# A graph kernel's attention messages: plain scatter into rows sorted by source block, summed by one-hot matmuls, in place of accumulating scatters

## The reference

```python
agg = segment_sum(xt[rel, src], dst)                 # both relational layers
...
scores = einsum(q[src], k[tgt]) / sqrt(16) + (curv @ Wc + bc)
probs  = segment softmax of scores over the edges of one tgt
messages = (probs[:, :, None] * v[tgt]).reshape(E, 128)
out = zeros_like(x).at[src].add(messages)            # sum by SOURCE node
out = out @ Wo + bo
x = x + out;  x = x + relu(LN(x) @ W1 + b1) @ W2 + b2
```

## Time and profile before

| | |
|---|---|
| device time, 3 runs | 12659.14 us median (12644.38 to 12664.75) |
| profiled execution, first to last instruction | span 10613.6 us |
| median less span | 2045.5 us |
| busy in the span | PE 57%, PEld 49%, DVE 53%, ACT 22%, POOL 70% |
| DMA | 851.83 MB, mean 80 GB/s |

### The profile page before, as it was taken

The page is one execution under the profiler, slowest core; times in us unless marked ns, Lnnn a source line. Parts: engine busy times, 40 slices in busy tenths (PEclk is TensorE's granted clock), DMA queues, the critical chain, the costliest instruction groups (busy, mean ns, idle before and its releaser), DMA issues. The chain is left out here.

```text
span 10613.6 us, 158173 instructions
## 1 busy us (share of the span) xinstructions
PE 6021.4 (57%) x25681; PEld 5185.3 (49%) x25682; DVE 5665.5 (53%) x14970; ACT 2361.1 (22%) x6137; POOL 7417.5 (70%) x6720
## 2 busy tenths in 40 slices
PE   0544444446444444434888898865666666666646
PEld 0333333333333333333888888854555555555544
DVE  5333333333333333335888888886555555555538
ACT  0100000001000000002555555532222222222222
POOL 1477777773777777761777777756888888888870
PEclk9655555556555555556555555556666666666667
DMA  1821111123111111112555555534555554444444
GB/s 38 292 71 52 52 52 52 52 52 132 52 52 52 52 52 52 52 52 80 136 136 136 135 137 135 136 92 62 58 58 59 59 59 58 59 59 59 58 58 120
DMA packets 1001820, 851.83 MB, mean 80 GB/s; under 512 B 187420, under 2 KB 892572, under 8 KB 1001707
## 3 DMA queue, kind: packets, MB, share of 16 engines
q0 software_dynamic: 400608, 439.19, 23.9%
q1 hardware_dynamic: 521299, 350.81, 11.7%
q10 hardware_dynamic: 79872, 61.39, 2.4%
HBM read 636.48 MB, written 234.17 MB: 82 GB/s over the span
## 5 line engine op out<-in xcount | busy, mean ns | idle before, releaser
L553 POOL DMA_INDIRECT stage_msg<-xt,stage_index x3328 | 3194.9, 960 | 1334.7 <-issue 924.8
L568 PE MATMUL stage_ps_agg<-stage_hot,stage_msg 128*128 128x128 f32 x6656 | 1714.7, 439 | 2522.8 <-DMA stage_msg<-xt,stage_index 2291.1
L1285 POOL DMA_INDIRECT sums<-big,stage_index x1664 | 2578.4, 1550 | 656.9 <-issue 397.0
L568 PEld LDWEIGHTS stage_ps_agg<-stage_hot,stage_msg 128*128 128x128 f32 x6656 | 1481.7, 328 | 2756.8 <-DMA stage_msg<-xt,stage_index 1402.2
L591 DVE TENSOR_TENSOR big<-big,stage_ps_agg 128x128 f32 x3328 | 957.8, 288 | 2388.6 <-PE stage_ps_agg L568 1985.0
L922 POOL DMA_INDIRECT big<-q,stage_index x1664 | 1600.0, 962 | 752.8 <-issue 443.0
L543 ACT ACTIVATE stage_index<-big 128x4 int32 x832 | 170.8, 205 | 4027.7 <-PE stage_ps_agg L568 4008.1
L1323 PE MATMUL stage_ps_val<-nodes_a,big 128*128 x3328 | 834.0, 430 | 332.7 <-ACT big L1267 216.9
L1357 DVE TENSOR_TENSOR big<-stage_ps_val,stage_prob 128x512 f32<-128x512 f32 x416 | 287.7, 692 | 1273.7 <-PE stage_ps_val L1323 1272.4
L1323 PEld LDWEIGHTS stage_ps_val<-nodes_a,big 128*128 128x128 f32 x3328 | 714.6, 317 | 381.8 <-issue 381.8
L1311 PE MATMUL stage_ps_src<-ident,stage_srcs 128*128 128x128 f32 x1664 | 367.8, 360 | 885.9 <-ACT stage_srcs L1256 750.5
(11 more groups left out here) (220 smaller groups left out, 7852.7 us busy)
## 6 DMA issues: line engine op xcount, KB each, us to landing
big<-in_edge_attr_dram SPq DMA_DIRECT2D x1664, 64.0 KB
xt<-big SPq DMA_DIRECT2D x26, 2048.0 KB, 6.6
stage_msg<-xt,stage_index POOLq DMA_INDIRECT x3328
stage_trow<-targets ACTq DMA_DIRECT2D x416, 128.0 KB
stage_trow<-targets SPq DMA_DIRECT2D x416, 128.0 KB, 3.3
sums<-stage_zero SPq DMA_DIRECT2D x104, 256.0 KB
big<-q,stage_index POOLq DMA_INDIRECT x1664
sums<-big,stage_index POOLq DMA_INDIRECT x1664
```

What stands on the lines that cost most here:

```text
L553: pool.indirect_dma_start(msg[q][:, j, :], None, xt, bass.IndirectOffsetOnAxis(ap=index[q][:, j:j + 1], axis=0))\
L568: last = nc.tensor.matmul(ps[q % 2][:, j, :], msg[q][:, j, :], hot[q % 2][:, j, :], start=True, stop=True)
L1285: pool.indirect_dma_start(d["sums"][h * G + j], bass.IndirectOffsetOnAxis(ap=index[q][:, j:j + 1], axis=0), total[q][:, j * D:(j + 1) * D] ...
```

## The change

1. **Slots.** Each valid or padding edge gets a row of its own in a DRAM table `slots` (212,992 rows of 528 B: 128 values, the source's number, three zeros). The edges are taken in 8 parts of 52 groups; within a part, rows are sorted by source block (`src >> 7`, 49 blocks). The first `aggregate` counts the edges of each block for each group, the second computes each edge's row; both load a broadcast list of blocks (`lanes`) once for each group.
2. **Plain scatter.** Messages go straight from DVE into `total`, whose rows POOL writes with four plain indirect transfers to a group. The search for repeats, the matmul within the tile and the copy are gone.
3. **Sums.** When a part has landed, SP loads its rows back, 5 tiles of 128 rows to a set, 52 sets to a part; a (tile, block) pair that straddles is loaded twice. PE multiplies each tile with a one-hot matrix of places in the block, DVE adds the five results to two accumulators in SBUF. This runs beside the groups of the next part, 56 groups behind (FIRST); the last part's 52 sets and four more turns follow the last group.
4. **Tables** that say which tile and block each load has are made on DVE and PE in groups 4 to 15 of `scatter`.
5. **Moves.** The loads of `targets`, `exp` and `marks` go from SP's queue to ACT's. `finish` takes the two accumulators from SBUF with two accumulating matmuls. The clearing of `sums` is gone.

```diff
+PARTS = 8
+GP = GROUPS // PARTS            # 52
+SET = 5
+LAG = SLOTS
+FIRST = GP + LAG                # 56
+SETS = PARTS * GP               # 416
+ROW = D + 4
 def aggregate(...):   # SP
-            for r in range(REP):
-                for a in range(BATCHES):
-                    sp.dma_start(d["sums"][r][...], zero[:, :]).then_inc(s_zd, 16)
+            if x.live(-SLOTS):
+                sp.wait_ge(s_counted if first else s_own, x.at(-SLOTS) + 1)
+            sp.dma_start(lanes[q][:, :], d["buckets"][...].partition_broadcast(W)).then_inc(s_lanes[q], 16)
+        if first:
+            for h in range(H):
+                sp.dma_start(d["marks"]...[:, h, :], d["tile_marks"]).then_inc(s_mk, 16)
+        walk(sp, group, 0, 0)
 # aggregate, DVE, in each group
+                if first:
+                    v.wait_ge(s_lanes[q], x.turn() * 16 + 16)
+                    nc.vector.tensor_scalar(met[h][:, :], lanes[q][:, :], t["lane"][0:W, :], 0.0, ALU.is_equal,
+                                            ALU.add, accum_out=t["counts"][:, bass.ds(x.at(), 1)])
+                else:
+                    nc.vector.tensor_tensor_scan(run[h][:, :], ones[:, :], own[h][:, :],
+                                                 begin[:, bass.ds(x.at(), 1)], ALU.mult, ALU.add)
...
+                    nc.vector.tensor_tensor(pick[h][:, :], run[h][:, :], own[h][:, :], ALU.mult)
 # scatter, SP
+        def load(y):
+            if y.live(-SLOTS):
+                sp.wait_ge(s_sum, y.at(-SLOTS) + 1)
+            r = windows(nc, mybir.EngineType.SP, pair_row, y.at() * SET, SET, K - 1)
+            for j in range(SET):
+                sp.dma_start(rows[q][:, j, :], d["slots"][bass.ds(r[j] * P, P), :]).then_inc(s_rows[q], 16)
+        for a in range(PARTS):
+            for q in range(SLOTS):
+                sp.wait_ge(s_sc[q], at[q] + (a + 1) * (GP // SLOTS) * (16 * G))
 # scatter, POOL
-                pool.indirect_dma_start(d["sums"][h * G + j], ..., total[q][:, j * D:(j + 1) * D], None,
-                                        compute_op=ALU.add).then_inc(s_sc[h], 16)
+                    pool.indirect_dma_start(d["slots"], ..., total[q][:, j, :], None).then_inc(s_sc[q], 16)
 # scatter, PE
-                for j in range(G):
-                    last = nc.tensor.transpose(ps_q[h][...], srcs[h][:, j:j + 1].to_broadcast([P, P]), ...)
-                for j in range(G):
-                    last = nc.tensor.matmul(ps_o[h][...], same[x.slot(-1)][:, j, :], msg[h][...])
+                for j in range(SET):
+                    last = nc.tensor.matmul(ps_s[h][:, j * P:(j + 1) * P], rows[q][:, j, 0:D], hot[h][:, j, :])
 # scatter, DVE
-                nc.vector.tensor_tensor(same[...], of_tiles(ps_q[h][:, :]), srcs[h]..., ALU.is_equal)
-                nc.vector.tensor_scalar(away[h]...)
-                nc.vector.tensor_tensor(dup, same[...], t["earlier"]..., ALU.mult)
-                nc.vector.tensor_reduce(dups[h]...)
-                nc.vector.scalar_tensor_tensor(moved[h]...)
-                nc.vector.tensor_tensor(dest[...]...)
+            if x.sums(1):
+                nc.vector.tensor_tensor(place[h][:, :], rows[q][:, :, D], pair_off[...], ALU.subtract)
+                v.wait_ge(s_place, x.at(1) + (1 - FIRST))
+                nc.vector.tensor_tensor(hot[h][:, :, :], t["iota"]..., place[h]..., ALU.is_equal)
+            if x.sums(-1):
+                w = windows(nc, mybir.EngineType.DVE, pair_window, (x.at(-1) - FIRST) * SET, SET)
+                v.wait_ge(s_sum, x.at(-1) + (1 - FIRST))
+                for j in range(SET):
+                    into = sums[j % 2][:, bass.ds(w[j] * P, P)]
+                    if j >= 2:
+                        v.wait_ge(s_acc, (x.at(-1) - FIRST) * SET + (j - 1))
+                    nc.vector.tensor_tensor(into, into, ps_s[h][:, j * P:(j + 1) * P], ALU.add)
 # finish, PE
-                    last = nc.tensor.matmul(ps_a[...], ot[:, j, :], wo_sb[:, :], start=True, stop=True)
+                    for c, sums in enumerate((t["nodes_b"], t["nodes_c"])):
+                        last = nc.tensor.matmul(ps_a[...], sums[:, ...], wo_sb[:, :], start=(c == 0), stop=(c == 1))
```

More of the change, by code:

```diff
@@ L501, in walk, with __init__, within, edge @@
         body(Group(g // slots, g % slots, slots, groups))
-def aggregate(nc, m, t, d, zero_sums):
+class Spot(Group):
+    def __init__(self, i, q, near):
+        super().__init__(i, q, SLOTS, None)
+        self.near = near
+    def within(self, k, lo, hi):
+        return lo <= self.near + k < hi
+    def edge(self, k=0):
+        return self.within(k, 0, GROUPS)
+    def live(self, k=0):
+        return self.edge(k)
+    def sums(self, k=0):
+        return self.within(k, FIRST, LAST)
+    def fixed(self):
+        return isinstance(self.i, int)
+def walk_edges(engine, body, marks, reach, lead):
+    g = marks[0] - reach
+    for a, b in zip(marks, marks[1:]):
+        first, end = -(-(a + (reach if a else lead)) // SLOTS), (b - reach) // SLOTS
+        if end - first < 2:
+            continue
+        for e in range(g, first * SLOTS):
+            body(Spot(e // SLOTS, e % SLOTS, e))
+        with engine.Fori(first, end) as i:
+            for q in range(SLOTS):
+                body(Spot(i, q, first * SLOTS + q))
+        g = end * SLOTS
+    for e in range(g, marks[-1] + reach):
+        body(Spot(e // SLOTS, e % SLOTS, e))
+def aggregate(nc, m, t, d, first):
     index = [m.sb(f"index{q}", [P, G], I32) for q in range(SLOTS)]
@@ L546, in _ @@
+        walk(act, group, 0, 0 if first else 6, peeled=1 if first else 2)
+        if not first:
+            act.wait_ge(s_kept, GROUPS)
     @block.gpsimd
@@ L560, in _, with group @@
         pe.sem_inc(s_freed, SLOTS)
-        with pe.Fori(0, TURNS) as i:
-            for q in range(SLOTS):
-                g = i * SLOTS + q
-                pe.wait_ge(s_hot, g + 1)
-                pe.wait_ge(s_read, g + 1)
-                pe.wait_ge(s_msg[q], i * (16 * G) + (16 * G + at[q]))
+        if not first:
+            pe.wait_ge(s_link, 1)
+            nc.tensor.matmul(ps_first[0:W, 0:PARTS], t["before"][0:W, 0:W], t["part_count"][:, :],
+                             start=True, stop=True).then_inc(s_first, 1)
+            pe.wait_ge(s_ones, 2)
+        def group(x):
+            if x.live():
+                q = x.slot()
+                pe.wait_ge(s_hot, x.at() + 1)
+                pe.wait_ge(s_read, x.at() + 1)
+                pe.wait_ge(s_msg[q], x.turn() * (16 * G) + (16 * G + at[q]))
                 for j in range(G):
@@ L570, in _ @@
                 last.then_inc(s_freed, 1)
+            if not first and x.live(-2):
+                h = x.slot(-2, 2)
+                pe.wait_ge(s_pick, x.at(-2) + 1)
+                if x.live(-4):
+                    pe.wait_ge(s_kept, x.at(-4) + 1)
+                for j in range(G):
+                    last = nc.tensor.matmul(ps_slot[h][:, j:j + 1], pick[h][:, j * P:(j + 1) * P], one[:, :],
+                                            start=True, stop=True)
+                last.then_inc(s_slot, 1)
+        walk(pe, group, 0, 0 if first else 2)
     @block.vector
@@ L1293, in _ @@
-        walk(pool, group, 0, 0)
-        for h in range(2):
-            pool.wait_ge(s_sc[h], TURNS * 2 * 16 * G + at[h])
+            if x.edge():
+                q = x.slot()
+                pool.wait_ge(s_index, x.at() * 2 + 2)
+                ring_index(pool, s_msg, x.at() + 1, passed)
+                for j in range(G):
+                    pool.indirect_dma_start(d["slots"], bass.IndirectOffsetOnAxis(ap=index[q][:, j:j + 1], axis=0),
+                                            total[q][:, j, :], None).then_inc(s_sc[q], 16)
@@ L1297, in _ @@
+        walk_edges(pool, group, (0, GROUPS), 0, SLOTS)
+        for q in range(SLOTS):
+            pool.wait_ge(s_sc[q], TURNS * 16 * G + at[q])
     @block.tensor
@@ L1336, in _ @@
-        walk(pe, group, 1, 1)
+            if x.sums():
+                h, q = x.slot(0, 2), x.slot()
+                pe.wait_ge(s_rows[q], x.turn() * (16 * SET) + (1 - FIRST // SLOTS) * (16 * SET))
+                pe.wait_ge(s_hot, x.at() + (1 - FIRST))
+                if x.sums(-2):
+                    pe.wait_ge(s_acc, (x.at() - (FIRST + 1)) * SET)
+                for j in range(SET):
+                    last = nc.tensor.matmul(ps_s[h][:, j * P:(j + 1) * P], rows[q][:, j, 0:D], hot[h][:, j, :],
+                                            start=True, stop=True)
+                last.then_inc(s_sum, 1)
@@ L1515, in batch @@
                 last.then_inc(s_y, 1)
-        walk(pe, batch, 1, 0, 2, BATCHES)
+        for g in range(-1, BATCHES):
+            batch(Group(g // 2, g % 2, 2, BATCHES))
     @block.gpsimd
@@ L1634, in build @@
             "xl": nc.dram_tensor("xl", (NP, D), FP32).ap(),
-            "sums": [nc.dram_tensor(f"sums{r}", (NP, D), FP32).ap() for r in range(REP)],
+            "slots": nc.dram_tensor("slots", (K * P, ROW), FP32).ap(),
         }
```

499 lines of the change are left out of this document (301 added, 198 removed).

## The result

The changed kernel takes 12940.5 us (median of 4), the kernel before 12651.8 beside it: ratio 1.0215, 95% interval 1.0176 to 1.0255, 2% slower. Forecast were 12175 us and a range of 11900 to 12620.

What follows compares the result with a forecast made beforehand. POOL was taken to bound `scatter` alone and `aggregate` by a thin margin. Terms -816 (scatter), +243 (tail), +45 and +105 (aggregates), -5 (prepare), -56 (finish) sum to -484: 12175 us, range 11900 to 12620.

Steps and rivals of the forecast that it cites:

- The ground: Whole kernel: profiled span 10613.6 us against a median of 12659.1; the 2045.5 us between them carried over unchanged.
- the sum: Whole kernel: -816 + 243 + 45 + 105 - 5 - 56 = -484 us, giving span 10130 and time 12175 us.
- Scatter, -816: `scatter` loop: plain writes at 1.0 us make DVE the bound, 5.5 us to a group; 2271 us in place of 3087.
- First aggregate, +45: First `aggregate`: `lanes` waits behind the copies of `marks`, so POOL stops after about six groups; +45 us, between 0 and 80.
- Second aggregate, +105: Second `aggregate`: DVE's added scan and product slow gathers that start inside them; +105 us, 20 or 310 at the ends.
- DVE's chain in my sum: Second `aggregate`: scan, `pick`, `hot` and four additions take DVE 4.85 us to a group, barely below POOL's 5.06.
- Tail, +243: After the last group of `scatter`: 52 sets served by SP at 4.5 us each, 234 plus 9; 190 or 260 otherwise.
- Finish, -56: `finish`: batches at 14.4 us in place of 18.24, and -7 for the first batch; -56 us, -30 to -110.
- A: Rival: POOL paces everything, `scatter` at 5.06 us to a group; total -735, 11925 us; chance 0.15.
- B: Rival: a plain write in `scatter` costs 1.27 us, 6.3 us to a group; -134, 12525 us; chance 0.14.
- C: Rival: indices on a write's DRAM side cost 1.55 us, not the addition; `scatter` stays at 7.42; +332, 12990 us; chance 0.12.

Runs made afterwards that it cites:

- the free run: The changed kernel, unchanged, a third time, where nothing stalls, beside the kernel before: 10300.3 us against 10609.0, ratio 0.9701.
- run 22060: Not a run's number: 22060 counts packets in the free run, the changed kernel, unchanged, against the kernel before: 10300.3 us, ratio 0.9701.

## Why the prediction was wrong

**The ground.** The step that failed is the first: "The 2045.5 us between them I carry over unchanged; no row shows what lies in them." They lay in the loops: 534 and 556 us in the two `aggregate` stages, 900 in `score`. So the earlier trace rows gave the pace of loops that the timed executions did not have, and a stage that was free of stalls before was taken to stay free. The new `scatter` did not stay so: 3160 us stalled, 2384 free. Without this error the sum would still have been too good, -298 us of span for -484, by the terms that follow.

**Scatter, -816.** Measured: +73 stalled, -701 free. The mechanism holds where nothing stalls: plain writes at 1.0 us, DVE the new bound, its register reads ahead of the additions. The size is 5.81 us for 5.5; the missed term is the read of five words, 1.20 us where I had taken the 0.34 of four. It is partly given back by the additions, which follow at 0.22 us, not 0.29, and by the steps before `hot`, 1.77 us and not 2.04. Of the first 56 groups, those from the 16th on went at 5.06 us, below the 5.2 of the sum, and the 12 in which the tables are made at 6.47. Stalled, the period is 7.76. Old `scatter` had 7.42 us of POOL's work to a group; the new one puts 42 instructions on DVE's queue and 28 on SP's (19.5 and 11 before), most of them register work, and both queues stall. Removing SP's reads, DVE's and both gives 0.1, 0.4 and 1.07 us of the 1.95 that the stalls cost; the rest is not traced to one queue.

**First aggregate, +45.** +57 stalled, +83 free; the stop came as told, but was 66 us stalled and 59 free for 50. At 83 us the term lies just beyond the 80 that I gave as its end.

**Second aggregate, +105.** +102 free, and by its mechanism: the gathers that meet DVE's longer operations go from a mean of 962 to 1023 ns (forecast 1.02 us). In free executions, before and after:

```profile
L553 POOL DMA_INDIRECT stage_msg<-xt,stage_index x1663 | 1599.1, 962 | 635.8 <-issue 465.7 <-ACT stage_index L543 170.1
L648 POOL DMA_INDIRECT stage_msg<-xt,stage_index x1663 | 1700.9, 1023 | 635.9 <-issue 437.9 <-ACT stage_index L618 198.0
```

The section on who interferes with whom of the page "SBUF — State Buffer" in the Trainium skill says that a VectorE instruction with two SBUF inputs contends with a GpSimd instruction that reads SBUF. The 962 and 1023 ns agree with it. The terms of DVE's chain in my sum add to 4.34 us, not to the 4.85 written there; both lie below POOL's 5.06, so nothing hung on it. Stalled the new operations cost nothing (-6 us): the group loses its 1.3 us with and without them, and POOL has time to spare.

**Tail, +243.** 298 us stalled, 288 free, each from the last group's writes on. The reason is that above: SP's read takes 1.07 us, a set 5.5 to 5.7 and not 4.5. Tail and `finish` together are +241 and +231 for the +187 of the sum.

**Finish, -56.** 292 us, from the last group's writes on, to 236 us after the tail: right in sum. A batch takes 16.1 us, not 14.4 (the 13 begin from 12710.4 to 12903.2), against the 18.24 of the earlier trace rows; the shorter start before the first batch gave the rest.

**Rivals.** A's condition (DVE under 5.06 us) and B's price (1.27 us) did not come. C's number, 12990, is close to the measured one by chance: its mechanism fell with the write of 0.997 us. The page "DMA: Bandwidth & Descriptors" in the Trainium skill, in the section on SWDGE against HWDGE and iDMA, prefers packets of at most 4096 bytes; from it I had estimated that rows of 528 B may need 16 packets and 0.085 us more. Here they did not: between 8000 and 9000 us of the free run 22060 packets serve 689 writes, 32 each like the gathers, and such a write took 1.004 to 1.010 us on the mean, against 0.997 for rows of 512 B.

**What stays open** is what stalls the queues. Shown: it comes and goes for the same program and chip; it strikes DVE's, SP's, PE's and sometimes ACT's queue, SP's also where it reads no registers; fewer instructions on DVE lessen it in `aggregate` (1.24 to 0.83 us to a group), fewer on SP don't in `score`; it is no cost of a turn, and a shift of 64 instructions does not move it. The old `scatter` never had it: no register, check or branch instruction over 0.4 us on any queue between 9600 and 12200 us of its stalled execution. Why the old one was spared and the new one not isn't known. And since free and stalled executions were met and not chosen, that stalls alone turn the gain of 298 us into a loss of 329 rests on the traces of both kinds, not on an edit that switches them off.

## What to carry to other kernels

Before a sum is made from a profile, hold its span against the timed median: a gap of 16% says that the profile is of another kind of execution, and every pace read from it is in doubt. Do not take it that a rewritten stage keeps the good behaviour of the one that it replaces: the old `scatter`, with 19.5 and 11 instructions to a group on DVE's and SP's queues, had no stalls in any profiled execution, the new one, with 42 and 28, has them. So count instructions on each queue, checks and register work too, and drop those that nobody needs (-3% in stalled executions of the old kernel, -3% in free ones of the new). Let tables read into registers begin each read at a multiple of four words.

## What was not expected of the hardware

- Queues of DVE, SP and PE stall in bursts of instructions of 0.69 to 0.73 us each; the same kernel took 12627 and 10609 us on one chip at two times.
- A register read of four words at a multiple of four takes 0.34 us on DVE, of five at such a place 0.59 to 0.65, of five elsewhere about 1.20; on SP 0.30, 0.52 and 1.07.
- An accumulating indirect write of 128 rows takes 1.543 us at the median, a plain one 0.958 (1.0 on the mean), a gather 0.945; in packets 144, 32 and 32.
